# Transformer stack with mixtures of experts: the capacity-bound experts work on whole rows, and their results are scattered to the tokens' places

## The reference

```python
x = x + L0_attn_a(layernorm(x))      # heads of 16, decay       "decay"
x = x + L0_ffn(layernorm(x))         # small experts            "experts1"
x = x + L0_attn_b(layernorm(x))      # heads of 16, rotary      "rope"
x = x + L0_ffn(layernorm(x))         # small experts            "experts2"
x = x + L1_attn_a(layernorm(x))      # one head of 256, causal  "causal"
x = x + L1_ffn(layernorm(x))         # large experts            "experts3"
x = x + L1_attn_b(layernorm(x))      # heads of 16, rotary      "latent"
x = x + L1_ffn(layernorm(x))         # large experts            "experts4"

def L1_ffn(x):                       # E = 8 experts, 256 -> 1024 -> 256
    probs = softmax(x @ Wr); e = argmax(probs); p = max(probs)   # one expert for a token
    rank = number of earlier tokens with the same expert
    keep = rank < 512                                            # capacity 4096 / 8
    y[token] = p * relu(x[token] @ W1[e]) @ W2[e] if keep else 0
```

## Time and profile before

| | us |
|---|---|
| median of 3 runs | 3227.94 (3222.7 to 3231.23) |
| profiled execution, its own time | 3217.11 |
| profiled execution, span of the trace | 3215.4 |
| PE busy | 2644.4 (82%) |
| DVE busy | 1911.3 (59%) |
| ACT busy | 1497.1 (47%) |
| POOL busy | 784.3 (24%) |
| granted TensorE clock, mean | 0.897 |

### The profile page before, as it was taken

One profiled execution on the slowest core, in us unless ns is written; L12 is line 12 of the kernel. 1 busy time (PEld: TensorE's weight loads), 2 busy tenths in 40 slices (PEclk: granted clock), 3 DMA queues, 4 the chain that ended last, 5 costly groups with the idle time before them and its releaser, 6 DMA issues. The chain is left out here.

```text
span 3215.4 us, 40264 instructions
## 1 busy us (share of the span) xinstructions
PE 2644.4 (82%) x12988; PEld 1373.2 (43%) x12988; DVE 1911.3 (59%) x4987; ACT 1497.1 (47%) x2906; POOL 784.3 (24%) x742
## 2 busy tenths in 40 slices
PE   4869999997567999999665885998399999976993
PEld 2324444444442333333443565666133333354662
DVE  3858888884438788887433543111788888832112
ACT  1457767776224766666612331111167767731110
POOL 0313323310333322331133103000434433212003
PEclk6789999998787999999877895999599999977996
DMA  7565555541354322232143003231423322212223
GB/s 239 171 211 163 163 157 158 163 120 45 110 160 120 111 90 90 80 100 60 61 148 109 1 1 115 79 118 68 134 80 104 115 89 90 80 70 83 105 93 116
DMA packets 213575, 351.31 MB, mean 109 GB/s; under 512 B 21192, under 2 KB 168265, under 8 KB 208632
## 3 DMA queue, kind: packets, MB, share of 16 engines
q1 hardware_dynamic: 197864, 299.06, 29.3%
q0 software_dynamic: 15504, 49.68, 4.7%
HBM read 203.24 MB, written 154.80 MB: 111 GB/s over the span
## 5 line engine op out<-in xcount | busy, mean ns | idle before, releaser
L1568 DVE CUSTOM_DVE_ANT_0 decay_junk<-decay_scores_q,decay_corr 128x512 bf16<-128x512 f32 x512 | 338.6, 684 | 118.9 <-PE decay_scores_q L1309 117.1
L1483 ACT ACTIVATE decay_probs<-decay_scores_k 128x512 f32<-128x512 f32 x512 | 294.8, 597 | 207.4 <-PE decay_scores_k L1328 168.5
L1571 DVE TENSOR_REDUCE rope_mx<-rope_scores_q 128x1 f32<-128x512 f32 x512 | 334.0, 685 | 90.5 <-PE rope_scores_q L1309 90.1
L1483 ACT ACTIVATE rope_probs<-rope_scores_k 128x512 f32<-128x512 f32 x512 | 294.6, 600 | 167.1 <-PE rope_scores_k L1322 165.8
L1571 DVE TENSOR_REDUCE latent_mx<-latent_scores_q 128x1 f32<-128x512 f32 x512 | 330.3, 684 | 67.1 <-PE latent_scores_q L1309 66.7
L1483 ACT ACTIVATE latent_probs<-latent_scores_k 128x512 f32<-128x512 f32 x512 | 294.9, 600 | 151.5 <-PE latent_scores_k L1322 149.8
L1309 PE MATMUL decay_scores_q<-decay_KS,decay_QS 96*128 96x512 bf16 x512 | 205.6, 402 | 47.2 <-DVE decay_mx L1568 34.5
L1309 PE MATMUL latent_scores_q<-latent_KS,latent_QS 96*128 96x512 bf16 x512 | 201.4, 395 | 49.0 <-DVE latent_mx L1571 32.5
L1309 PE MATMUL rope_scores_q<-rope_KS,rope_QS 96*128 96x512 bf16 x512 | 201.3, 395 | 21.5 <-DVE rope_mx L1571 12.7
L1322 PE MATMUL latent_scores_k<-latent_QS,latent_KS 99*128 99x512 bf16 x512 | 197.3, 387 | 6.0 <-ACT latent_probs L1483 3.6
L1322 PE MATMUL rope_scores_k<-rope_QS,rope_KS 99*128 99x512 bf16 x512 | 197.2, 387 | 4.5 <-ACT rope_probs L1483 2.7
(11 more groups left out here) (396 smaller groups left out, 5315.6 us busy)
## 6 DMA issues: line engine op xcount, KB each, us to landing
decay_parts_dram<-decay_parts SPq DMA_DIRECT2D x64, 384.0 KB, 3.0
decay_KS<-decay_parts_dram SPq DMA_DIRECT2D x64, 384.0 KB, 6.1
decay_QS<-decay_parts_dram SPq DMA_DIRECT2D x64, 384.0 KB, 6.7
decay_parts_dram<-decay_parts SPq DMA_DIRECT2D x64, 256.0 KB, 3.1
experts3x_w<-in_w_dram SPq DMA_DIRECT2D x16, 1024.0 KB, 7.3
experts4x_w<-in_w_dram SPq DMA_DIRECT2D x16, 1024.0 KB, 7.2
experts_xin<-dispatched SPq DMA_DIRECT2D x96, 128.0 KB, 2.5
results<-experts_y SPq DMA_DIRECT2D x96, 128.0 KB
```

Source lines behind the costliest of these rows:

```text
L1483: act.activation(probs[:, (b * 16 + kk) % PSLOTS, h, :], psB[:, s % 2, :], ACT.Exp, scale=scale).then_inc(exp_done, 1)
L1568: dve.tensor_tensor_reduce(junk[:, a % 2, :], psA[:, A_BANK[k], :], corr[:, qt, :], 1.0, -3.0e38, ALU.mult, ALU.max, mx[:, grp % 2, qt, h: ...
L1571: dve.tensor_reduce(mx[:, grp % 2, qt, h:h + 1], psA[:, A_BANK[k], :], AX.X, ALU.max).then_inc(a_done, 1)
```

## The change

The buffer `X` becomes `rows`, 264 floats for a token: the 256 of X, mean and variance, the reciprocal root and the root, the gate probability (`GATE`), two token numbers (`TOKEN`, `TOKEN_LAST`) and one float unused. `X`, `MV` and `RSTD` are views of it for all other layers. In a large-experts layer:

- `dispatch` scatters these rows, 1056 bytes each, in place of normalised ones of 1024 bytes. The rows of the buffer that no token fills hold a token number out of range.
- SP copies X (in `experts3` with its two statistics, 1032 bytes a row) at the start of the layer to a DRAM buffer `next_rows`, or in `experts4` to the output: 8 DMAs, semaphore `kept`.
- The gate probability is computed in each of the four pieces of the routing (`over`, `sums`, `gated`), not at its end.
- In the loop DVE normalises the loaded tokens into a new tile `xnn` (`normal_tokens`), for expert e+1 between its relus f=5 and f=7 of expert e, and PE's `turn` waits for that. DVE's copy of a finished piece is now one operation that reads PSUM, the gate and the raw token and writes x + gate * result to `y`; in `experts3` statistics follow it.
- POOL scatters each finished piece of 128 rows by its token numbers to `next_rows` or to the output, 32 indirect DMAs. The store to `cap_ye`, the buffer itself, and the 32 gathers by token go away.
- SP issues the weights of expert e when PE has finished outer(e-2), and the tokens of expert e only when the four scatters of expert e-2 have landed (`sent`).
- The `latent` layer loads X and statistics from `next_rows` by 8 plain DMAs of SP (`Rows.load`), the first ahead of its other loads. Its DVE stream has no adds and no statistics, and ACT waits for the loads.

```diff
-            if last_layer:
-                for p in range(2):
-                    pool.wait_ge(y_stored[p], 16 * (E // 2))
-                for q in range(NB):
-                    results.gather(pool, q)
+            pool.wait_ge(kept, 16 * NB)
+            for e in range(E):
+                for t in range(QT):
+                    pool.wait_ge(y_added if last_layer else y_done, e * QT + (t + 1))
+                    pool.indirect_dma_start(
+                        out=to, out_offset=bass.IndirectOffsetOnAxis(ap=xin[:, e % 2, t, token:token + 1].bitcast(I32), axis=0),
+                        in_=y[:, e % 2, t, 0:WIDTH], in_offset=None, bounds_check=T - 1, oob_is_err=False).then_inc(
+                            sent[e % 2], 16)
...
             for p in range(2):
                 weights(p, p)
+            for q in range(NB):
+                keep_rows = to[4 * q * P:(4 * q + 4) * P, :].rearrange("(t p) d -> p t d", p=P)
+                sp.dma_start(keep_rows, rows[:, 4 * q:4 * q + 4, 0:WIDTH]).then_inc(kept, 16)
             sp.wait_ge(scattered, 16 * NT)
             for p in range(2):
                 tokens(p, p)
-            for j in range(E // 2 - 1):
-                for p in range(2):
-                    e = j * 2 + p
-                    store(e, p)
-                    weights(e + 2, p)
-                    tokens(e + 2, p)
+            for e in range(2, E):
+                sp.wait_ge(y_ready, (e - 2) * QT + QT)
+                weights(e, e % 2)
+                sp.wait_ge(sent[e % 2], 16 * QT * (e // 2))
+                tokens(e, e % 2)
+            sp.wait_ge(kept, 16 * NB)
             for p in range(2):
-                store(E - 2 + p, p)
-            for p in range(2):
-                sp.wait_ge(y_stored[p], 16 * (E // 2))
-            if last_layer:
-                for q in range(NB):
-                    sp.wait_ge(added, 4 * q + 4)
-                    sp.dma_start(ins["out"][q], X[:, 4 * q:4 * q + 4, :]).then_inc(out_stored, 16)
-                sp.wait_ge(out_stored, 16 * NB)
+                sp.wait_ge(sent[p], 16 * QT * (E // 2))
...
             def turn(j, p):
-                pe.wait_ge(x_loaded[p], j * 16 + 16)
                 n = j * 2 + p
+                pe.wait_ge(xnn_ready, n * QT + QT)
...
+            def normal_tokens(e):
+                dve.wait_ge(x_loaded[e % 2], e // 2 * 16 + 16)
+                if e >= 2:
+                    dve.wait_ge(t_ready, 2 * e - 2)
+                for t in range(QT):
+                    dve.tensor_scalar(xnn[:, e % 2, t, :], xin[:, e % 2, t, 0:D], xin[:, e % 2, t, D:D + 1],
+                                      xin[:, e % 2, t, RSTD_COL:RSTD_COL + 1], ALU.subtract, ALU.mult).then_inc(xnn_ready, 1)
+
             def relus(j, p):
                 n = j * 2 + p
                 for f in range(1, FC, 2):
+                    if f == 7 and n + 1 < E:
+                        normal_tokens(n + 1)
                     dve.wait_ge(h_ready, n * FC + (f + 1))
...
-                    dve.tensor_copy(y[:, p, t, :], psY[:, t % 2, 0:D]).then_inc(y_taken, 1)
...
+                    dve.scalar_tensor_tensor(y[:, p, t, 0:D], psY[:, t % 2, 0:D], xin[:, p, t, GATE:GATE + 1],
+                                                   xin[:, p, t, 0:D], ALU.mult, ALU.add).then_inc(y_added, 1)
+                    if last_layer:
+                        continue
+                    dve.wait_ge(y_added, n * QT + (t + 1))
+                    dve.bn_stats(st[:, t, :], y[:, p, t, 0:D]).then_inc(y_stats, 1)
+                    dve.wait_ge(y_stats, n * QT + (t + 1))
+                    dve.bn_aggr(y[:, p, t, STATS], st[:, t, :]).then_inc(y_done, 1)
...
         def _(sp):
+            if late_rows:
+                results.load(sp, 0)
             for name, src in ins["load"]:
                 sp.dma_start(tiles[name][:], src).then_inc(loaded_by[name], 16)
+            if late_rows:
+                for q in range(1, NB):
+                    results.load(sp, q)
```

178 lines of the change are left out of this document (93 added, 85 removed).

## The result

The changed kernel takes 3153.76 us (median of 4 runs, 3150.06 to 3158.03), the kernel before beside it 3227.19 us (4 runs): ratio 0.9775, with an interval of 0.9757 to 0.9793. That is 73.4 us less; 80.8 were forecast, as 3147 us. Run again later beside the kernel before, on one of the three chips of the experiments, it gave 0.9769 (0.9754 to 0.9784).

What follows compares the result with a forecast made beforehand. PE bounds the expert loops, POOL's gathers the kernel's end, DVE's stream the start of `latent`. -49.5 - 34.6 + 3.3 = -80.8 us from the median 3227.94 gives 3147 us, own range 3132 to 3163, wider range 3128 to 3172.

Steps and rivals of the forecast that it cites:

- The end of the kernel, -49.5: After DVE's last piece, gathers, adds and stores give way to one scatter: -49.5 us, or -47.4 with a 3.43 us landing.
- The start of `latent`, -34.6: Border of `experts3` and `latent`: without adds in DVE's stream, first maximum at 2281.6 in place of 2316.24, -34.6 us.
- bounds of -28.7 and -37.7: Start of `latent`: -28.7 us if DVE's standstill comes back, -37.7 if scores come with DVE at 2278.5.
- The heads, +3.3: Head of each large layer: PE waits for four normalisations and rows are longer, +3.3 us for both layers.
- The loops, 0: Loop over experts: tokens land at T + 7.2 to 10.0, in time with 2.5 us to spare, so 0 us.
- threshold of T + 12.5: Loop: tokens there by T + 12.5 cost PE no wait, T being the end of outer(e-2).
- Rival A: Loop: tokens come late behind POOL's scatter, PE waits 2.5 us in 12 passes, +30: 3177 us; chance 0.10 short of slower.
- Rival B: Start of `latent` gains 6 to 15 us less, by DVE's standstill or delayed parts: 3153 to 3162 us; chance 0.08 beyond the range.
- C: Dispatch: a row over 1024 bytes costs POOL a second descriptor, up to 27 us a layer, about 3200 us; chance 0.05.
- The rule weighed against the change: Token loads: rows off 256-byte boundaries need some 14% more beats; first loads 0.2 us more each, sum -80.2 us.
- D: Loop: slower than before if scatter and load need 18 us, perhaps by DVE locking GpSimd out of a shared port; chance 0.03.
- The signs that I named: Changed profile: end within 5 us of PE's last matmul, `latent` maximum at 39 us, passes 28.6 us, dispatch DMAs near 0.98 us.

Runs made afterwards that it cites:

- adds_back: Changed kernel with the adds and statistics of sequences 1 to 7 put back into DVE's stream of `latent`, no gathers: 3165.39 us, ratio 0.9837.
- gathers_back: Changed kernel with 32 gathers put back on POOL's queue in `latent`, nobody waiting for them: 3156.57 us, ratio 0.9804.
- tokens_late: Changed kernel with two small waited-for loads ahead of each load of tokens in the loop: 3188.54 us, ratio 0.9881.

## Why the prediction was right

The gain lay where it was forecast, and came out 7 us smaller than the 80.8 forecast. Both ends missed one term, what POOL does at the end of a block, and in the loop one landing was mis-sized without a cost.

- **The end of the kernel, -49.5.** Measured -45.0. The terms up to POOL hold: 0.48 of the multiply-add, then POOL from 3145.44, 1.28 us behind DVE's start (1.25 forecast), 0.97 of the DMA, 1.4 of landing. The step that failed is "with 0.5 us that I allow for the end of the program": from POOL's end to the end of the span it is 6.2 us, of which the drain hides the landing and takes 5.3. No row stood behind those 0.5 us. The bound of -47.4 did not hold it either, since it varied the landing and not the end of the block.
- **The start of `latent`, -34.6.** Measured -30.5, inside the bounds of -28.7 and -37.7. The failing step is the same: the layer begins 7.3 us behind DVE's last piece, where the sum 0.77 + 0.98 + 1.32 gave 3.1. Behind it the order is as forecast, with PE's scores as the last releaser, and so is the length, 35.0 us from the first load to the first maximum (35.2). The length is in part luck: root 4.4 us behind the issue of the row load (3.7 forecast), first scores 11.4 us behind the write of the parts (12.85), and first maximum 0.65 us behind the first scores, for which I had nothing. The claim that DVE's stream and not POOL's gathers ended last is borne out by `adds_back` for 20 of the 30 us; `gathers_back` shows that gathers had a price of their own, larger than the 1.9 us that I gave them.
- **The heads, +3.3.** Measured +2.5 (1.3 and 1.2, where I had 1.65 each).
- **The loops, 0.** Right, but with 0.4 us of cover in `experts3` and not "2.5 us to spare". The mis-sized term is the landing of the scatter, 5.5 us beside the weights where I had 1.32 to 3.43 from rows with nothing ahead of it; the weights of that sum were in my text, as traffic beside the load, and not ahead of the scatter. The threshold of T + 12.5 was right (`tokens_late`: T + 12.4). Rival A named just this, with 6 us as the landing from which it starts. It was half a microsecond away, so that it stayed out was luck and not the margin that I had worked out.
- **Rival B** (latent gains less by 6 us or more) did not come; **C** neither: rows of 1056 bytes leave POOL at 0.98 us, with the same gap, as the chain's rows at the end of the dispatch show.

```profile
2901.19 0.98 POOL cap_dispatched L52
2902.17 0.30 issue
2902.48 2.33 DMA cap_dispatched<-X,experts_slot
...
2904.83 3.84 DMA experts4x_xin<-cap_dispatched
```

- **The rule weighed against the change.** The first load of tokens takes 3.84 us with the longer rows, 3.63 in the earlier trace rows: 0.21 us more, the 0.2 that I put (3% more bytes alone are 0.11). By the rule in the Trainium skill ("DMA: Bandwidth & Descriptors", "How a descriptor splits into AXI transactions") it would have been some 0.5, an estimate from the 14% more beats. No such extra shows: while the two first loads of `experts3` flow, the DMA engines move 366 to 408 GB/s with the longer rows and 374 to 398 before.
- **D and its port.** The scatters, beside DVE's operations, stay at 0.97 us each, so nothing was seen of a lockout.
- **The signs that I named.** Two of them came out beyond their limits, both by the drain: the end is 8.5 us and not within 5 behind PE's last matmul, and the first maximum is 43.5 us and not 39 behind the start of DVE's last piece (the parts leave at 31.4, not 26.5). The others held: no wait of PE in the passes, 28.6 us each, and 0.98 us for a row of the dispatch.
- **Slips in the sums.** "6.7 to 9.5" in rival D should be 6.7 to 8.8, and -37.7 and -28.7 with 0.2% on either side give 3138 to 3159, not 3132 to 3163. Neither changes the forecast.

## What to carry to other kernels

Before an engine is made the last one of a block, look in the trace for what it does behind its last instruction: a drain that was hidden behind slower engines is a term of the sum. A landing time read from an empty queue must not be used where megabytes are issued just ahead; find out what is in front of the DMA. Small loads that somebody waits for can be ordered ahead of large ones that nobody does, which here took 4 us off a landing and nothing off the time. And work removed from a serial stream of one engine is worth its full duration only at the place where that stream ends last; here a run with only this work put back gave 19.9 us where 19.8 were expected.

## What the runs showed of the hardware that I had not expected

- POOL's DRAIN at the end of a block with indirect DMAs: over 5.3 us behind the last of them at both borders of the changed kernel, 2.7 us behind the dispatch in `experts3` of before, and 5.4 us long when it starts with all of them landed.
- An indirect write of 128 rows lands 1.3 to 1.6 us behind POOL's end with free queues, 4.8 to 5.7 us with 2.1 MB of plain loads issued up to 2 us ahead. A section of the Trainium skill's "DMA: Bandwidth & Descriptors", "SWDGE vs HWDGE vs iDMA", says that the two kinds of DMA stand in different queues of an engine, which takes them in turn. In this trace the indirect write was not through before the loads ahead of it.
- PE, after standing for 2.4 to 3.5 us, in three of six passes came back at a granted clock of 0.89 over the next 15.4 us, so part of that stretch at the lower of its levels of 1.2 and 2.4 GHz, and `outer` took 1.7 us more; in the other three it was 1.00. Which it was did not go by the length of the stand (2.84, 3.54 and 3.00 us against 2.44, 3.07 and 2.73).
- One chip ran the kernel before in 3139.83 us where the others took 3215.34 to 3227.19, some 2.5% less. Of the first trace's time 60 to 80 us were missing ahead of `experts3`, in stages that no kernel here changed, and why stays open.
- Eight loads of half a megabyte in a row took SP 6.99 us to issue, 0.87 each, where one alone took 0.38, and a load of two floats a partition issued behind them kept ACT waiting for 9.65 us.
